# Two VectorE steps are put in front of the maxima's copies: Q's second low part in slot two, the first norm's sum in slot three

## What is computed

```python
h1 = n1_w * arcsinh(x) + n1_b
h  = x + na2d(h1)                 # 8 heads of 32, each query looks at its 3x3 neighbours (clamped at the edge)
h2 = n2_w * arcsinh(h) + n2_b
out = h + gelu(h2 @ mlp_w1 + mlp_b1) @ mlp_w2 + mlp_b2

def na2d(h1):
    q, k, v = split(h1 @ qkv_w + qkv_b)     # q scaled by 32 ** -0.5
    attn = softmax(q . k[3x3 neighbours])
    return (attn . v[3x3 neighbours]) @ proj_w + proj_b
```

## Time and profile before

| | us |
|---|---|
| median of 3 runs | 4439.54 (4438.06 to 4439.81) |
| the profiled execution's own time | 4440.94 |
| its span, first to last instruction | 4439.1 |
| mean granted TensorE clock | 0.992 |

### The profile page before, as it was taken

How to read it: one execution, slowest core, us unless ns; L and a number is a source line. 1 busy time by engine, 2 the same in 40 slices (tenths; PEclk the granted TensorE clock), 3 DMA queues, 4 the chain that set the end, 5 groups by cost and what they waited for, 6 DMA issues and landing times.

```text
span 4439.1 us, 129514 instructions
## 1 busy us (share of the span) xinstructions
PE 4159.5 (94%) x49224; PEld 2857.8 (64%) x49224; DVE 3926.1 (88%) x8225; ACT 3631.7 (82%) x5377; POOL 3359.0 (76%) x4092
## 2 busy tenths in 40 slices
PE   5999999999999999999999999999999999999997
PEld 3666666666666666666666666666666666666664
DVE  6899999989989998998999899899989989999984
ACT  4888888888888888888888888888888888888884
POOL 2777777777777777777777777777777777777775
PEclk8999999999999999999999999999999999999998
DMA  4555555555555555555555555555555555555551
GB/s 120 132 141 139 142 139 143 136 139 141 141 140 140 142 137 139 141 140 141 140 142 137 140 141 139 140 141 141 139 139 144 136 140 140 141 141 138 142 133 50
DMA packets 644105, 607.94 MB, mean 137 GB/s; under 512 B 77070, under 2 KB 639376, under 8 KB 639888
## 3 DMA queue, kind: packets, MB, share of 16 engines
q1 hardware_dynamic: 643488, 599.66, 51.2%
HBM read 206.02 MB, written 135.40 MB: 77 GB/s over the span
## 4 chain that ended last, share of the span: by engine, by line
DVE 42%; PE 18%; POOL 13%; issue 13%; ACT 12%; SPq 1%; DMA 0%; POOLq 0%; DVEq 0%; ACTq 0%
PE ps L381 16%; POOL b_lo L1163 6%; POOL b_hi L1161 6%; DVE ps L841 5%; DVE queries L860 5%; DVE o_norm L874 4%; DVE ln_u L767 4%; DVE ln_u L760 4%; DVE k_nat L815 4%; ACT L1073 4%; DVE ln_u L763 3%; DVE h L802 3%; ACT p_hi L1064 3%; DVE q_nat L808 3%; ACT prob L1063 2%
## 5 line engine op out<-in xcount | busy, mean ns | idle before, releaser
L1146 POOL TENSOR_TENSOR p_lo<-prob,p_hi 100x512 f16<-100x512 f32 x1024 | 1269.7, 1245 | 619.1 <-ACT p_hi L1064 619.1
L1063 ACT ACTIVATE prob<-ps 100x512 f32<-100x512 f32 x1024 | 610.2, 596 | 51.1 <-PE ps L381 49.3
L874 DVE TENSOR_TENSOR o_norm<-ps,recip 64x128 f32<-64x128 f32 x2048 | 590.2, 288 | 49.3
L1172 POOL TENSOR_TENSOR g_lo<-g,g_hi 128x512 f16<-128x512 f32 x512 | 593.8, 1160 | 41.0
L1064 ACT ACTIVATE p_hi<-ps 100x512 f16<-100x512 f32 x1024 | 616.4, 602 | 0.0
L381 PEld LDWEIGHTS ps<-v_win,p_hi 100*128 100x128 f16 x8192 | 476.0, 98 | 204.7 <-issue 66.9
L381 PE MATMUL ps<-w_hi,g_hi 128*128 128x256 f16 x2048 | 561.1, 274 | 0.0
L841 DVE TENSOR_REDUCE ps<-ps 128x8 f32<-128x800 f32 x512 | 509.1, 994 | 58.6 <-PE ps L381 54.2
L381 PE MATMUL ps<-w_lo,g_hi 128*128 128x256 f16 x2048 | 560.9, 274 | 0.0
L381 PE MATMUL ps<-w_hi,g_lo 128*128 128x256 f16 x2048 | 560.8, 274 | 0.0
L381 PE MATMUL ps<-v_win,p_hi 100*128 100x65 f16 x8192 | 515.6, 193 | 27.0 <-POOL p_lo L1146 18.4
(11 more groups left out here) (100 smaller groups left out, 11497.9 us busy)
## 6 DMA issues: line engine op xcount, KB each, us to landing
keys<-k_win SPq DMA_DIRECT2D x1536, 100.0 KB, 2.3
v_win<-v_rows SPq DMA_DIRECT2D x1024, 101.6 KB
queries<-q_nat SPq DMA_DIRECT2D x1536, 64.0 KB
v_rows<-v_nat SPq DMA_DIRECT2D x256, 260.0 KB, 4.3
xin<-in_x_dram SPq DMA_DIRECT2D x128, 512.0 KB, 4.3
out_dram<-y SPq DMA_DIRECT2D x256, 256.0 KB, 3.0
queries<-in_query_mask_dram SPq DMA_DIRECT2D x128, 224.0 KB
keys<-in_mlp_w_dram SPq DMA_DIRECT2D x2, 512.0 KB, 6.5
```

The source lines that it names most:

```text
L874: s = v.tensor_tensor(o_norm[r, c], av[r, :, HD * e:HD * e + HD], recip[c % 2][r].to_broadcast([NQ, PAIRS, HD]), ALU.mult)
L1063: act.activation(prob[b][0:NK], ps[0:NK, B_ST + b, :], ACT.Exp, scale=INV * INV).then_inc(prob_ready, 1)
L1146: pool.tensor_tensor(p_lo[b][0:NK], prob[b][0:NK], p_hi[b][0:NK], ALU.subtract).then_inc(p_lo_ready, 1)
L1172: pool.tensor_tensor(g_lo[:, m, :], g32[:, m, :], g_hi[:, m, :], ALU.subtract).then_inc(g_lo_ready, 1)
```

## The change

Only the order of DVE's queue changes. No instruction is added or taken out, no wait is edited. In slot two `q_low(t + 2, par, 1)` is issued in front of `maxima_to_queries` and no longer behind it. In slot three `sum1_(t + 3)` is issued in front of `maxima_to_queries` and no longer behind it.

```diff
@@ -933,6 +933,10 @@
                     if att:
                         sum_reciprocal(t, 2 * k)
                         normalise(t, 2 * k)
+                    if k == 1 and pre:
+                        q_low(t + 2, par, 1)
+                    if k == 2 and fill:
+                        sum1_(t + 3)
                     if more:
                         maxima_to_queries(ta, par if ta == t else old, ka)
 
@@ -941,8 +945,6 @@
                     if k == 0 and post:
                         h_from_projection(t - 1, old, (u - 1) % XT, 0)
                         h_from_projection(t - 1, old, (u - 1) % XT, 1)
-                    if k == 1 and pre:
-                        q_low(t + 2, par, 1)
                     if k == 1 and fill:
                         x_from_transposes(t + 3, (u + 3) % XT, 0)
                         x_from_transposes(t + 3, (u + 3) % XT, 1)
@@ -950,8 +952,6 @@
                         sum2_(t - 1)
                     if k == 1 and pre:
                         v_low(t + 2, 0)
-                    if k == 2 and fill:
-                        sum1_(t + 3)
                     if k == 2 and fin:
                         result(t - 2, 0)
```

## The result

| | before | after |
|---|---|---|
| median, us | 4438.8 (4438.04 to 4439.81, 4 runs) | 4549.02 (4548.35 to 4551.06, 4 runs) |
| the profiled execution's span, us | 4439.1 | 4547.5 |
| mean granted TensorE clock | 0.992 | 0.991 |

The changed kernel is slower by 2.5%: the ratio is 1.0249, with a 95% interval of 1.0233 to 1.0264. The forecast was 4540 us with a range of 4500 to 4575.

A forecast was written before the change was run, and what follows sets the result against it. Bound: a loop of waits through DVE, POOL, PE and ACT. Slot two 0, slot three 125 x 0.81 = 101 us; 4440.9 + 101 = 4542, median 1.4 below: 4540 us, range 4500 to 4575.

The forecast's parts named there:

- The main step: Slot three: sum1 issued 0.8 earlier waits behind POOL's b_lo half 0, ends unchanged at 2027.89; copies delayed 2.28.
- The length alone: DVE's sum without port conflict: estimated at 1.08 + 0.14 = 1.22 us.
- the sum takes the port first: Slot three: root precedes b_lo half 0, sum runs 2025.64 to 2026.86; -0.08 a step, 4430 us; chance 0.10 with no conflict.
- the case of no conflict: Slot three: port doesn't bind, sum ends at 2027.03; -0.07 a step, 4430 us; chance 0.10 shared with port taken first.
- The cover on PE: PE before scores_t 6: all but 1.27 of the copies' 2.28 delay covered; new wait of 0.9 to 1.3.
- The term: Slot three's loss at PE's mlp_in 3, after old waits for b_lo and GELU are used up: +0.81 a step.
- Q's low part: Slot two: moving q_low in front of the copies counts 0; the other end was -27 us.
- The part about the 0.22: Slot two: second xT starts 0.22 earlier, but sign2, held behind p_lo 5, still ends at 2024.90; gain swallowed.
- the 0.08: DVE, slot two: back-to-back instructions overlap by some 0.08, so q_low takes 0.67 of the queue.
- The rule from the Trainium skill's page: Port wait: blocked engine resumes about 115 ns after the other's end; sum about 0.25 later, some 4571 us.
- b_hi half 1 never got in front of the waiting sum: Rival, slot three: b_hi half 1 takes the port first, sum ends at 2028.44; 1.36 a step, 4610 us; chance 0.04.
- Nothing behind mlp_in gave anything back: Rival: something waiting behind mlp_in absorbs part of the delay; half of it would give 4490 us; chance 0.06.

The follow-up runs named there:

- e1: Kernel before with only sum1_ moved in front of the copies, q_low 1 left behind them in slot two: 4532.7 us.
- e7: The changed kernel with the first norm's sum replaced by a tensor_reduce, root and division left out: 4448.2 us.
- e4: Kernel before with sum1_ in front of the copies and POOL's b_lo half 0 additionally waiting for the sum: 4493.1 us.
- e6: Kernel before with q_low 1 and both x_from_transposes in front of slot two's copies, and sum1_ in front of slot three's: 4423.1 us.
- e5: Kernel before with q_low 1 and both x_from_transposes in front of slot two's copies, slot three as before: 4430.5 us.
- e3: The changed kernel with the first norm's sum replaced by a strided tensor_scalar reading one tensor, root left out: 4550.7 us.

## Why the prediction was right, and where its sizes were off

**The port and the place of the sum.** The main step held to the hundredth. The forecast let the sum be issued at 2025.73 to 2025.81 behind b_lo half 0 and end 1.08 after it. In e1, where slot two is as before, it is issued at 2025.80 and ends at 2027.88. The length alone, 1.22, was worked out by letting POOL release the port as early as VectorE does. The trace of before bears it out with a sum beside which POOL is idle:

```profile
2018.15 1.22 DVE L763 SCALAR_TENSOR_TENSOR ln_u<-ln_u,ln_s 128x1024 f32<-128x1024 f32 x1
```

In e1 the log on ACT still waits 2.22 for it, b_hi half 1 is still 1.60. e7 and e4 show the cause by experiment, e6 the rival "the sum takes the port first", to which the forecast gave 0.10 together with the case of no conflict: it occurs when the root is early enough.

**The cover on PE.** Expected in front of scores_t was a wait of 0.9 to 1.3, and it is 1.10 in the changed kernel and in e1. The wait for b_lo (0.32 in the forecast's working) and for the GELU (0.14) were swallowed as expected, the group of b_hi has 3.5 us of waiting left. The term came out as 0.74 instead of 0.81. In e1 scores_t starts 0.01 earlier than forecast. scores_t and scores take 1.05 up to mlp_in (2007.90 to 2008.95) where the forecast shifted the 1.09 of the earlier trace rows. From half 1 to mlp_in 3 it is 3.66 (2009.61 to 2013.27), where the forecast shifted 3.68 (2029.65 to 2033.33). That is the 0.07.

**Q's low part.** This is the step that failed, though the total stayed inside the range. Taken was 0, with -27 us as the other end, and measured is +0.134 a step, some 17 us: outside both ends. The part about the 0.22 was right (the second xT follows at once, the gain stays behind p_lo 5, sign2 is 1.79 long). The mis-sized term is the length of the queue in front of the first xT. The forecast moved q_low with its 0.67 as it stood between the copies and xT and had the first xT unchanged at 2016.71, but the 0.08 by which the next instruction starts before q_low's end doesn't exist for a copy. The copies were to end at 2016.68 and end at 2016.80 (2034.18 less 17.38). In every step they begin 0.03 after the end of what stands in front of them. 0.12 later at xT is 0.13 later at V, at p_lo 5, at sign2's end (2025.03, was 2024.90), at the root and at b_lo half 0. So the forecast's reason for taking 0, that p_lo 5 "does not move", is what fell.

**The sum.** 0.738 and 0.134 make 0.872, the change has 0.852, and 0.852 x 125 = 107 us, where the forecast had 101. The spans of the profiled executions differ by 108 us, the medians by 110; the 3 us between are not explained here. The errors went against each other: a term 0.07 too large, a term 0.13 that was missing. That the total is within 9 us of the median is in part luck. The step's length was given as 34.54, it is 34.585.

**What did not happen.** The rule from the Trainium skill's page "SBUF — State Buffer", section "A bandwidth-pool intuition that's wrong", by which a blocked engine goes on some 115 ns after the other's end would have made the sum 0.25 longer than it is. That page of the Trainium skill gives its figure for a DMA whose descriptors GpSimd has to write behind a VectorE copy; the forecast carried it over to two compute instructions. In the change and in e1 the sum ends 1.08 to 1.09 after b_lo in every step, as before. Against a length of 1.22 alone that is a release 0.14 ahead of POOL's recorded end. b_hi half 1 never got in front of the waiting sum. Nothing behind mlp_in gave anything back.

## What to carry to other kernels

Before moving a VectorE instruction with two SBUF inputs or a tensor_scalar on SBUF, look which GpSimd instruction runs at the new place and which of the two starts first: issued behind it, it ends 1.08 us after GpSimd's (for 1024 elements, as here), and everything put behind it in the queue pays. Look for what the moved instruction was waiting on by then; one that is issued earlier but can't end earlier only stands in the way of the short instruction that other engines wait for. And to a queue's sum belong the overlaps of neighbours, which change with the neighbour.

## What the runs showed that was not expected

**A copy doesn't start in its predecessor's tail.** q_low (0.75 long) is followed by xT after 0.67 and by the copies after 0.78. Over all steps the copies start 0.03 after the end of o_norm, of q_low, of the sum and, in e5, of xT, and what follows a copy and need not wait also starts 0.03 after its end. Behind instructions of 512 columns from PSUM any other successor that need not wait starts some 0.08 before their end. But the pair alone doesn't settle it: `v_low` starts 0.08 before sum2's end where sum2 follows xT (before), and 0.03 after it where sum2 follows the copies (e5, e6). Whether it is the copy's form, its eight partitions or its semaphore is open.

**A fixed late start in each eighth step.** Where the sum has to wait for ACT's root, it starts 0.10 after the root's end in most steps and 0.45 after it in 15 of the 124, always eight steps apart (change, e1, e3, e4, e7; the row of e7 above is such a one: 2031.69 to 2032.16). In the change this costs nothing, since the port keeps the sum waiting longer anyway. In e4 and e7 such steps are 0.35 longer (e7: 34.08 and not 33.73). The other steps of e7 are as long as those of before, so the late starts are all that it loses against before. The cause is open.

**The port is decided within hundredths.** magnitude1 won by 0.02 in the earlier trace rows, the sum of e6 by 0.01 or less in every step, and 0.15 in the other direction cost 2.1% (e1).
